# The feed-forward part's first steps set among the convolutions' second round

## The chip, the core and the metric

One core of a Trainium2 chip (trn2) runs the whole kernel. Its engines are TensorE (PE; weight loads are shown apart as PEld), VectorE (DVE), ScalarE (ACT), GpSimd (POOL) and SyncE (SP, which issues the transfers here). The metric is the device time of one execution in microseconds (us), as a median of runs. The program is written by hand: each engine has one list of instructions in a fixed order, and counting semaphores hold an instruction until another engine's is done.

## The reference, cut to what matters

Two layers over x of 4 x 512 x 128 float32. Each has an attention-like part and a feed-forward part, both behind a layernorm with a scale and a shift taken from a small vector (`mod`). The change touches the seam between layer 0's two parts, and the place where layer 1's expert weights are multiplied by a rotation.

```python
h = _layernorm(x) * (1 + ca) + sa
x = x + ga * _L0_attn_ref(h, ...)      # two long convolutions with gates, by way of FFTs
h = _layernorm(x) * (1 + cb) + sb
x = x + gb * _L0_ffn_ref(h, ...)
...
# _L0_ffn_ref
sim = einsum('bthn,hkpn->pbthk', h @ W_q, keys)              # 2 x 4 heads x 64 keys
(sx, sy), (ix, iy) = top_k(sim, 8)                           # 8 best of each side
scores, pk = top_k(sx[..., :, None] + sy[..., None, :], 8)   # 8 best of 64 pairs
w = silu(einsum('btd,bthkd->bthk', h, down_embed[indices]) * softmax(scores))
experts_states = einsum('bthk,bthkd->btd', w, up_embed[indices])
dense = silu(h @ W_up.T) @ W_down.T
return dense + experts_states
...
# _L1_ffn_ref, behind its experts
for i in range(3): moe_out = moe_out @ expm(gens[i])
```

## The kernel before

**The convolutions.** `convolutions_tensor`, `_scalar`, `_gpsimd` and `_vector` handle one batch of 512 rows (four tiles of 128). Two lanes run side by side; lane 0 takes batches 0 and 2, lane 1 takes 1 and 3, so there are two rounds. A batch is transposed, projected (L848), folded (L913, L914), transformed (L857), multiplied by the filter's spectrum (L920 to L925) and transformed back (L866), twice; then it is added to `x` (L938, L940). Lane 0 owns PSUM banks 4 and 5, lane 1 owns 6 and 7.

**The rotations.** `rotations_tensor`, `_scalar` and `_vector` form the matrix exponentials of layer 1. At their heart are 16 products of three matrices on PE (L639, twelve matmul passes each), and after each a DVE step (L778) and ACT copies (L621, L624) that the next product waits for. A last pair of products with copies between (L670, L783, L787; L674, L791) gives the rotation. Then PE multiplies the expert weights by it in four groups (L684, and L688 for the bias) in banks 0 and 1, and DVE copies each group out (L796, L799).

**The order.** Each engine's list is made by `together`, which takes one piece in turn from each of its streams (lane 0, lane 1, setup, rotations) until all are used up; `yield` ends a piece, and `idle(n)` skips n turns:

```python
def together(*streams):
    streams = list(streams)
    while streams:
        for s in list(streams):
            if next(s, StopIteration) is StopIteration:
                streams.remove(s)
```

No clock and no cost enters: the place of a step is where its turn falls. On the chip the lists run as fast as the semaphores let them.

**The feed-forward part** (`feed_forward_*`) starts when these streams are used up. Ahead of its loop over 16 tiles stands a head. DVE takes the statistics of batch 0 (`statistics`, L1278 to L1283), POOL normalises it (`normalised`, L1222, L1227), PE transposes it (`turned`, L980), DVE scales and shifts it into `hT` (`keep_turned`, L1287). PE forms tile 0's similarities (`sim`, L997), the dense half's four up-projections (`up`, L988) and tile 1's similarities; ACT copies the similarities (L1119) and applies silu (L1113). DVE then chooses for tile 0: `tops_of` (L1301, eight best of 64), `indices_of` (L1307, L1310), `best_of` (L1316 to L1325), `strike` (L1330) and `code_of` (L1334 to L1353). ACT's `exps` (L1123, L1125) and POOL's `past_of` (L1234 to L1249) serve the same choice. PE's `logit` (L1029) and `down` (L1004) follow, then in the loop `code` (L1011, L1013) and `rank` (L1022, L1023), whose result with ACT's exponential (L1135) DVE turns into weights in `gate_of` (L1362, L1364), four heads to a tile. In the loop's turn n DVE does `tops_of` and `indices_of` of tile n + 1 ahead of tile n's gates. PE's banks are SIM 4, GD 5, SUMS 6, OUT 7, RANK 0 and 1, LOGIT 2 and 3.

## Time and profile before

| | before |
|---|---|
| median of 3 runs | 1162.44 us (1161.05 to 1164.18) |
| the profiled execution's own time | 1161.96 us |
| its span, first to last instruction | 1160.7 us |
| mean granted TensorE clock | 0.987 of full |
| convolutions and rotations | to about 121 us |
| feed-forward of layer 0, first gate (L1362) | 144.03 us |

The times are those of whole executions; span and rows come from one profiled execution. A row of the timeline has a start, a duration, the engine, the program's line and the operation, `x12` for twelve instructions merged in one row, and in brackets how long the engine stood idle before and what released it. Matmuls are pipelined and the rows hold their modelled ends, so two rows on PE may overlap: the distance from start to start is what one costs in a full stream. A pair of passes makes one float32 matmul, hence `x2` and `x12`. PEclk in the windows is the clock granted to TensorE, 1.00 for 2.4 GHz and 0.50 for 1.2 GHz.

### The profile page before, as it was taken

The page shows a single profiled execution, that of the slowest core. Times are in us where ns is not written, and L with a number is a line of the kernel's source. Part 1 is how long each engine was busy: PE and PEld are TensorE (multiplying, and loading weights), DVE is VectorE, ACT ScalarE, POOL GpSimd, SP SyncE. Part 2 cuts the span into 40 slices and gives each one's busy share as a digit, 9 for nine tenths or more (in the row PEclk, how much of TensorE's full clock was granted, in tenths as well). Part 3 has the DMA queues.
Part 4 walks back from the last instruction along what each step waited for, and adds up shares of the span by engine and source line. Part 5 has one row for each costly group of instructions (what it writes and reads, how often), then busy time and mean ns, then how long its engine had stood idle before and what let it go on. Part 6 is the DMA issues. An engine that isn't in the chain of part 4 may idle for free.

```text
span 1160.7 us, 23183 instructions
## 1 busy us (share of the span) xinstructions
PE 1090.5 (94%) x7601; PEld 792.8 (68%) x7617; DVE 937.8 (81%) x3329; ACT 697.2 (60%) x1800; POOL 421.2 (36%) x707
## 2 busy tenths in 40 slices
PE   6798679999998999999999999999999999999997
PEld 5688446666666767777777777777776777656766
DVE  3988699999989599788888888888888898756767
ACT  1254345555566656777676767676767777745441
POOL 4400322233324135444444444444444555422310
PEclk9999889999999999999999999999999999999999
DMA  9200300000000000000000000000000000000000
GB/s 280 55 2 1 110 1 1 1 1 1 2 1 1 2 1 2 1 2 1 2 1 1 2 1 2 2 1 1 2 1 2 1 2 2 2 1 5 11 7 17
DMA packets 19957, 15.33 MB, mean 13 GB/s; under 512 B 2432, under 2 KB 18816, under 8 KB 19712
## 3 DMA queue, kind: packets, MB, share of 16 engines
q1 hardware_dynamic: 19840, 13.86, 4.1%
q8 instruction: 63, 1.03, 0.4%
q14 instruction: 54, 0.44, 0.1%
HBM read 12.81 MB, written 1.05 MB: 12 GB/s over the span
## 4 chain that ended last, share of the span: by engine, by line
PE 76%; DVE 13%; ACT 5%; issue 3%; POOL 1%; DMA 0%; SPq 0%; DVEq 0%; ACTq 0%; POOLq 0%
PE bank L1607 12%; PE bank L1637 11%; PE bank L1601 10%; PE bank L1556 8%; PE bank L1044 5%; PE bank L1945 5%; PE bank L1966 4%; PE bank L1577 3%; PE bank L1585 3%; PE bank L1029 3%; ACT prb L1672 2%; PE bank L639 2%; DVE prob L1362 1%; PE bank L1023 1%; PE bank L1004 1%
## 5 line engine op out<-in xcount | busy, mean ns | idle before, releaser
L1703 POOL TENSOR_SCALAR prb<-prb,rnorm 128x512 f32<-128x512 f32 (+3 forms) x512 | 270.4, 545 | 349.4 <-DVE rnorm L1793 349.3
L1672 ACT ACTIVATE prb<-prb,negmax 128x512 f32<-128x512 f32 (+3 forms) x512 | 280.9, 552 | 113.5 <-DVE negmax L1775 113.5
L1775 DVE CUSTOM_DVE_ANT_0 prb<-bank,mask 128x512 f32<-128x512 f32 (+3 forms) x512 | 218.7, 484 | 18.5 <-PE bank L1601 18.3
L1607 PE MATMUL bank<-ident,prb 128*128 128x128 f32 x1280 | 158.2, 275 | 3.4 <-POOL prb L1703 2.9
L1607 PEld LDWEIGHTS bank<-ident,prb 128*128 128x128 f32 x1280 | 139.6, 141 | 22.9 <-issue 12.0
L1637 PE MATMUL bank<-prbT,vv 128*64 128x512 f32 (+3 forms) x1024 | 152.0, 439 | 0.0
L1637 PEld LDWEIGHTS bank<-prbT,vv 128*64 128x64 f32 x1024 | 63.4, 137 | 82.4 <-issue 82.2
L1680 ACT ACTIVATE prbT<-bank 128x512 f32<-128x512 f32 x128 | 76.5, 598 | 62.0 <-PE bank L1607 60.1
L1784 DVE COPY prbT<-bank 128x512 f32<-128x512 f32 x128 | 87.8, 690 | 14.8 <-PE bank L1607 14.4
L1672 ACT ACTIVATION_READ_ACCUMULATOR prb<-prb,negmax 128x1 f32 x512 | 96.8, 189 | 0.0
L2003 ACT ACTIVATE h<-bank,eb1T 128x512 f32<-128x512 f32 x64 | 43.7, 687 | 53.8 <-PE bank L1945 53.6
L1135 ACT ACTIVATE prob<-bank,negbest 128x512 f32<-128x512 f32 x64 | 43.9, 686 | 46.5 <-PE bank L1029 46.4
L2140 DVE SCALAR_TENSOR_TENSOR moe<-bank,wde,moe 128x128 f32<-128x128 f32 x128 | 44.8, 350 | 28.5 <-PE bank L1966 24.5
L1029 PE MATMUL bank<-mpair,hT 128*128 128x512 f32 x128 | 67.2, 607 | 0.1
L1044 PEld LDWEIGHTS bank<-ident,prob 128*128 128x128 f32 x512 | 59.1, 192 | 7.1 <-ACT gT L1113 5.5
L1945 PE MATMUL bank<-hTm,ew 128*128 128x512 f32 x128 | 61.0, 606 | 2.3 <-ACT h L2003 1.9
L1966 PEld LDWEIGHTS bank<-ew2R,h 128*128 128x128 f32 x512 | 58.9, 192 | 4.8 <-issue 4.3
L1044 PE MATMUL bank<-ident,prob 128*128 128x128 f32 x512 | 60.4, 276 | 0.7 <-ACT gT L1113 0.7
L1966 PE MATMUL bank<-ew2R,h 128*128 128x128 f32 x512 | 59.7, 276 | 0.0
L1362 DVE SCALAR_TENSOR_TENSOR prob<-bank,prob 128x512 f32<-128x512 f32 x64 | 43.8, 684 | 19.3 <-PE bank L1023 19.3
L1793 DVE RECIPROCAL rnorm<-rowsum 128x2 f32<-128x2 f32 (+1 forms) x192 | 31.7, 165 | 27.7 <-ACT prb L1672 27.6
L1364 DVE SCALAR_TENSOR_TENSOR prob<-prob,rsum,bank 128x512 f32<-128x512 f32 x64 | 47.8, 748 | 2.3
(465 smaller groups left out, 2368.7 us busy)
## 6 DMA issues: line engine op xcount, KB each, us to landing
x<-in_x SPq DMA_DIRECT2D x2, 512.0 KB, 6.0
ew2T<-in_ew2T SPq DMA_DIRECT2D x1, 1024.0 KB, 7.7
ew<-in_ew SPq DMA_DIRECT2D x1, 1024.0 KB, 5.6
wq<-in_Wq SPq DMA_DIRECT2D x2, 512.0 KB, 5.1
wk<-in_Wk SPq DMA_DIRECT2D x2, 512.0 KB, 7.6
wv<-in_Wv SPq DMA_DIRECT2D x1, 1024.0 KB, 8.2
out<-res SPq DMA_DIRECT2D x16, 64.0 KB, 1.5
wmod<-in_wmod SPq DMA_DIRECT2D x2, 384.0 KB, 6.9
```

The costliest lines, as they stand in the source:

```text
L1029: T.matmul(LOGIT[h % 2][:, :], tokens(n), mpair[:, h, :, :].rearrange("p i j -> p (i j)"), start=True, stop=True).then_inc(ff_logit, 1)
L1044: last = T.matmul(SUMS[:, c * P:(c + 1) * P], prob[n % 3][:, h, c * P:(c + 1) * P], ident[:, :], start=(h == 0), stop=(h == PH - 1 and c < 3))
L1556: last = T.matmul(into[:, :], left[:, j % 4, :], right, start=(n == 0), stop=(n == 2))
L1601: last = T.matmul(s_of(j, s, i, qc), q[r, qc * P:(qc + 1) * P], k[r, 0:(qc + 1) * P], start=(n == 0), stop=(n == 2))
L1607: last = T.transpose(into[:, at + (qc - kc) * P:at + (qc - kc + 1) * P], prb[j % 2][:, i, p_at[qc] + kc * P:p_at[qc] + (kc + 1) * P], iden ...
L1637: last = T.matmul(BO[DH * i:DH * i + DH, kc * P:S], vv[j // 4 % 2][:, kc, (2 * g + i) % 4, mp, :], prbT[:, i, pt_at[kc]:pt_at[kc] + (NT - ...
L1672: A.activation(v, v, ACT.Exp, scale=-1.0, bias=negmax[j % 2][:, place[qc], i:i + 1], accum_out=rowsum[j % 2][:, place[qc], i:i + 1]).then_ ...
L1703: last = G.tensor_scalar(v, v, rnorm[j % 2][:, place[qc], i:i + 1], 1.0, ALU.mult, ALU.mult)
L1775: V.tensor_tensor_reduce(prb[j % 2][:, i, p_at[qc]:p_at[qc] + (qc + 1) * P], s_of(j, s, i, qc), mask[:, (NT - 1 - qc) * P:S], 1.0, LARGEST ...
L1784: V.tensor_copy(prbT[:, part // 2, pt_at[1]:pt_at[1] + 4 * P], turn_bank(j, part)[:, :]).then_inc(at_ptv, 1)
L1945: T.matmul(F01[j % 2][:, :], ew1[:, j // HC, (j % HC) * P:(j % HC + 1) * P], hTm[b % 2], start=True, stop=True).then_inc(mx_up, 1)
L1966: last = T.matmul(bank[2 + t % 2 * 4 + e // 4][:, (e % 4) * D:(e % 4 + 1) * D], h1[b % 2][:, e * HC + c, t * P:(t + 1) * P], ew2R[:, e, c, ...
```

## The change

The head of the feed-forward part becomes a fifth stream, `ahead`, of each engine's `together`; the rest is `main`. Into `ahead` go: batch 0's statistics, rows, transposes and `hT` (now made by ACT, L1200, not DVE), the similarities of tiles 0 and 1, the four up-projections with their silus, the whole choice of tile 0, and `tops_of` and `indices_of` of tile 1. They use banks 2 and 3 (`AHEAD`), free after setup. `main` starts with `logit(0, 0)` and `down(0)`. ACT, not DVE, copies the rotated expert weights out of PSUM, and PE waits for the copies at the first `rank`. Tile buffers change places so that what `ahead` writes lies outside of the lanes' memory, and `main` waits for each lane's last batch (`cv_done`) where it takes over its memory or banks.

```diff
@@ convolutions_vector
-            dve.did(V.tensor_tensor(x[:, b, :, :], x[:, b, :, :], w.pv[:, :, 0, :], ALU.add))
-            dve.settle()
+            V.tensor_tensor(x[:, b, :, :], x[:, b, :, :], w.pv[:, :, 0, :], ALU.add).then_inc(w.cv_done, 1)
+            V.wait_ge(w.cv_done, n0 + 1)
@@ rotations_scalar, at its end (rotations_vector loses the same copies, L794 to L799)
+            yield from idle(6)
+            for j in range(E1 * HC // 4):
+                A.wait_ge(ew2_ps, j + 1)
+                A.activation(ew2R[:, 2 * j:2 * j + 2, :, :], bank[j % 2][:, :].rearrange("p (e c d) -> p e c d", e=2, c=HC), ACT.Copy).then_inc(ew2_kept, 1)
+                yield
+            A.wait_ge(ew2_ps, E1 * HC // 4 + 1)
+            A.activation(eb2R[:, :], bank[0][0:E1, 0:D], ACT.Copy).then_inc(ew2_kept, 1)
@@ feed_forward_tensor
+            def ahead():
+                yield from idle(32)
+                T.wait_ge(keys_ready, 1)
+                T.wait_ge(pre.ln_xhat, 1)
+                for t in range(NT):
+                    last = T.transpose(AHEAD[0][:, t * P:(t + 1) * P], pre.xhat[:, t, :], ident[:, :])
+                last.then_inc(pre.ln_ps, 1)
+                yield from idle(2)
+                T.wait_ge(layer0_in, LAYER0_IN)
+                T.wait_ge(pre.h_ready, 1)
+                sim_ahead(0)
+                up_ahead(0)
+                yield from idle(2)
+                T.wait_ge(ff_simk, 1)
+                sim_ahead(1)
+                T.wait_ge(ff_silu, 1)
+                up_ahead(1)
+                yield from idle(2)
+                T.wait_ge(ff_simk, 2)
+                up_ahead(2)
+                T.wait_ge(ff_silu, 2)
+                up_ahead(3)
+                yield
...
+            def main():
+                T.wait_ge(const_ready, 3)
+                T.wait_ge(ff_silu, NT)
+                T.wait_ge(lanes[0].cv_done, B // 2)
+                logit(0, 0)
+                down(0)
+                for n in range(TILES):
...
+                    if n == 0:
+                        T.wait_ge(ew2_kept, E1 * HC // 4 + 1)
+                    rank(n, 0)
...
+                    if n == 0:
+                        T.wait_ge(lanes[1].cv_done, B // 2)
@@ feed_forward_scalar
+            def ahead():
+                yield from idle(33)
+                A.wait_ge(pre.ln_ps, 1)
+                A.activation(hT[0], AHEAD[0][:, :], ACT.Identity, bias=modT[0][:, 3, 0:1], scale=modT[0][:, 4, 0:1]).then_inc(pre.h_ready, 1)
+                yield from idle(2)
+                keep_sim(0)
+                silu_up(0, 0)
+                yield from idle(2)
+                keep_sim(1)
+                silu_up(0, 1)
+                yield from idle(2)
+                silu_up(0, 2)
+                silu_up(0, 3)
+                yield from idle(4)
+                exps(0)
+                yield
@@ feed_forward_gpsimd
+            def ahead():
+                yield from idle(28)
+                normalised(pre, 0, 0)
+                yield from idle(13)
+                past_of(0)
+                yield
@@ feed_forward_vector
+            def ahead():
+                yield from idle(27)
+                V.wait_ge(const_ready, 3)
+                V.wait_ge(rows_kept, len(ROWS))
+                statistics(pre, 0)
+                yield from idle(9)
+                tops_of(0)
+                yield from idle(2)
+                at = indices_of(0)
+                yield from idle(2)
+                cast = best_of(0, *at)
+                yield from idle(2)
+                strike(0)
+                yield from idle(2)
+                code_of(0, cast)
+                yield from idle(2)
+                tops_of(1)
+                yield from idle(2)
+                found_first.extend(indices_of(1))
+                yield
+
+            def main():
+                for n in range(TILES):
...
+                    if more and n:
+                        tops_of(n + 1)
...
+                        at = indices_of(n + 1) if n else found_first
@@ tensor_program (the other engines alike)
-            together(batches(convolutions_tensor, 0), batches(convolutions_tensor, 1), setup_tensor(), rotations_tensor())
...
-            last = feed_forward_tensor()
+            ff_ahead, ff_main, last = feed_forward_tensor()
+            together(batches(convolutions_tensor, 0), batches(convolutions_tensor, 1), setup_tensor(), rotations_tensor(), ff_ahead())
+            ff_main()
```

How the lists change, at three places. A row is one instruction or a run of equal ones, output`<-`inputs. The numbers behind names count buffers.

PE, second round, the first forward transforms of the two lanes and the squarings between them (L639 before, L648 now); before:

```order
L857 MATMUL bank<-fold_78,c_fwd_sb 128x128 x8
L848 MATMUL bank<-proj_w,hT_1_90 128x384
L639 MATMUL bank<-xm_e 128x128 x6
L857 MATMUL bank<-fold_86,c_fwd_sb 128x128 x8
L639 MATMUL bank<-xm_e 128x128 x6
L866 MATMUL bank<-spec_o_81,c_inv_sb 128x128 x8
L639 MATMUL bank<-xm_e 128x128 x6
```

and now, the same place, with the similarities (L1084) and up-projections (L1087) between:

```order
L859 MATMUL bank<-fold_78,c_fwd_sb 128x128 x8
L850 MATMUL bank<-proj_w,hT_1_90 128x384
L1084 MATMUL bank<-msim,hT_101 128x512
L1087 MATMUL bank<-hT_101,w_up 128x512
L648 MATMUL bank<-xm_e 128x128 x6
L859 MATMUL bank<-fold_86,c_fwd_sb 128x128 x8
L1084 MATMUL bank<-msim,hT_101 128x512
L1087 MATMUL bank<-hT_101,w_up 128x512
L648 MATMUL bank<-xm_e 128x128 x6
L868 MATMUL bank<-spec_o_81,c_inv_sb 128x128 x8
L1087 MATMUL bank<-hT_101,w_up 128x512 x2
L648 MATMUL bank<-xm_e 128x128 x6
```

A similarity and an up-projection stand between the transforms and each of two squaring products, and two up-projections ahead of a third.

DVE, from the squaring step before lane 0's last multiplication by the filter; before:

```order
L778 SCALAR_TENSOR_TENSOR xm_e<-bank,xm_over,xm_b_120 128x128 x3
L920 TENSOR_TENSOR spec_o_81<-spec_79,filt 128x512
L921 TENSOR_TENSOR spec_t_80<-spec_79,filt 128x512
L924 TENSOR_TENSOR spec_o_81<-spec_o_81,spec_t_80 128x256
L925 TENSOR_TENSOR spec_o_81<-spec_o_81,spec_t_80 128x256
L778 SCALAR_TENSOR_TENSOR xm_e<-bank,xm_over,xm_b_120 128x128 x3
```

and now, where L1392 to L1411 are `code_of(0)` and L922 to L927 are L920 to L925 of before:

```order
L787 SCALAR_TENSOR_TENSOR xm_e<-bank,xm_over,xm_b_120 128x128 x3
L1392 TENSOR_TENSOR chosen<-pair_r,pair 128x256
L1396 TENSOR_TENSOR xeq<-iota_x,topf 128x256
L1400 TENSOR_REDUCE cnt<-chosen 128x32
L1401 TENSOR_TENSOR ycode<-iota_y,topf 128x2048
L1404 TENSOR_TENSOR xeq<-xeq,cnt 128x256
L1406 TENSOR_REDUCE esum<-ebest 128x4
L1409 TENSOR_REDUCE xcode<-xeq 128x32
L1411 RECIPROCAL rsum<-esum 128x4
L922 TENSOR_TENSOR spec_o_81<-spec_79,filt 128x512
L923 TENSOR_TENSOR spec_t_80<-spec_79,filt 128x512
L926 TENSOR_TENSOR spec_o_81<-spec_o_81,spec_t_80 128x256
```

The eight instructions of the code stand ahead of lane 0's last filter product, on which its last inverse transform waits.

PE, from the rotated expert weights on; before:

```order
L684 MATMUL bank<-xm_b_121,ew2T 128x128 x16
L688 MATMUL bank<-xm_b_121,eb2T 8x128
L980 MATMUL bank<-ident,xhat_pre 128x128 x4
L997 MATMUL bank<-msim,hT_93 128x512
L988 MATMUL bank<-hT_93,w_up 128x512 x4
L997 MATMUL bank<-msim,hT_93 128x512
L1029 MATMUL bank<-mpair,hT_93 128x512
L1004 MATMUL bank<-downT,hT_93 128x512
L1011 MATMUL bank<-rank_ident,ycode 128x128 x16
L1013 MATMUL bank<-identb,xcode 128x128
```

and now:

```order
L693 MATMUL bank<-xm_b_121,ew2T 128x128 x16
L697 MATMUL bank<-xm_b_121,eb2T 8x128
L1032 MATMUL bank<-mpair,hT_101 128x512
L1007 MATMUL bank<-downT,hT_101 128x512
L1014 MATMUL bank<-rank_ident,ycode 128x128 x16
L1016 MATMUL bank<-identb,xcode 128x128
```

Transposes, both similarities and the up-projections are gone from behind the rotated weights; `logit`, `down` and the code follow at once.

## Rows read from the trace of the kernel before

**Rows 1.** The page's first part, whole span: busy time, share, instructions.

```profile
PE 1090.5 (94%) x7601; PEld 792.8 (68%) x7617; DVE 937.8 (81%) x3329; ACT 697.2 (60%) x1800; POOL 421.2 (36%) x707
```

**Rows 2.** Waits, 74 to 145 us: who waited for whom, us, times, longest.

```profile
PE bank L980 <- POOL xhat_pre L1227: 6.3, 1, 6.3
```

**Rows 3.** Windows: length, busy PE, PEld, DVE, ACT, POOL, PEclk, DMA, GB/s.

```profile
78.56:98.97 20.41, 20.28 (x151) 18.07 (x152) 15.68 (x42) 10.37 (x28) 0.00 (x0) 1.00 0.00 1
98.97:115.38 16.41, 13.48 (x119) 13.07 (x117) 14.18 (x36) 6.05 (x15) 0.00 (x0) 1.00 0.00 1
115.38:144.03 28.65, 20.02 (x79) 12.10 (x81) 17.86 (x99) 8.40 (x14) 8.71 (x12) 0.82 0.37 111
```

**Rows 4.** Timeline of PE, the loop: start us, us, what, [idle before it].

```profile
78.56 1.58 PE L639 MATMUL bank<-xm_e 128*128 128x128 f32 x12 [0.36 <-ACT xm_b L624]
...
88.96 1.50 PE L639 MATMUL bank<-xm_e 128*128 128x128 f32 x12
...
92.64 1.58 PE L639 MATMUL bank<-xm_e 128*128 128x128 f32 x12
...
95.84 1.50 PE L639 MATMUL bank<-xm_e 128*128 128x128 f32 x12
...
98.97 1.50 PE L639 MATMUL bank<-xm_e 128*128 128x128 f32 x12
...
115.38 5.46 PE L684 MATMUL bank<-xm_b,ew2T 128*128 128x128 f32 x32 [2.55 <-DVE xm_b L791]
```

**Rows 5.** Timeline of PE, behind the loop.

```profile
120.77 0.39 PE L688 MATMUL bank<-xm_b,eb2T 128*8 128x128 f32 x2
127.50 1.09 PE L980 MATMUL bank<-ident,xhat_pre 128*128 128x128 f32 x4 [6.34 <-POOL xhat_pre L1227]
...
136.04 1.02 PE L997 MATMUL bank<-msim,hT 128*128 128x512 f32 x2
136.90 1.02 PE L1029 MATMUL bank<-mpair,hT 128*128 128x512 f32 x2
137.76 1.02 PE L1004 MATMUL bank<-downT,hT 128*128 128x512 f32 x2
139.89 1.21 PE L1011 MATMUL bank<-rank_ident,ycode 128*128 128x128 bf16 x16 [1.11 <-DVE xcode L1351]
...
142.12 0.38 PE L1023 MATMUL bank<-sel_x,codeT 128*128 128x512 bf16 x1
```

**Rows 6.** Timeline of DVE, feed-forward's beginning up to the first gate.

```profile
135.34 0.59 DVE L1316 MAX8 best<-pair 128x8 f32<-128x64 f32 x4
...
136.15 0.09 DVE L1330 MATCH_VALUE_LOAD pair_r<-best,pair 128x8 f32 x1
...
137.04 0.47 DVE L1334 TENSOR_TENSOR chosen<-pair_r,pair 128x256 f32<-128x256 f32 x1
...
139.84 1.08 DVE L1301 MAX8 tops<-sim 128x8 f32<-128x64 f32 x8
...
142.13 0.41 DVE L1307 TENSOR_TENSOR pair<-tops 128x256 f32<-128x256 f32 x1
...
144.03 0.66 DVE L1362 SCALAR_TENSOR_TENSOR prob<-bank,prob 128x512 f32<-128x512 f32 x1
```

**Rows 7.** Timeline of DVE, the copy that releases the rotated weights.

```profile
115.04 0.28 DVE L791 COPY xm_b<-bank 128x128 f32<-128x128 f32 x1
```

**Rows 8.** L920 by itself: count, duration ns min/median/max, first and last start, forms.

```profile
L920 DVE TENSOR_TENSOR spec_o<-spec,filt x8: 681/688/843, 36.8 to 107.5; 128x512 f32<-128x512 f32 x8
```

**Rows 9.** Windows of 2 us around the rotated weights' start (columns as above).

```profile
112.00:114.00 2.00, 0.49 (x2) 0.30 (x2) 1.93 (x5) 0.15 (x1) 0.00 (x0) 1.00 0.00 0
114.00:116.00 2.00, 0.62 (x4) 0.62 (x5) 1.93 (x6) 0.00 (x0) 0.00 (x0) 0.96 0.00 0
116.00:118.00 2.00, 2.00 (x12) 2.00 (x11) 1.34 (x2) 0.00 (x0) 0.00 (x0) 0.50 0.00 0
118.00:120.00 2.00, 2.00 (x14) 2.00 (x14) 0.70 (x2) 0.00 (x0) 0.00 (x0) 0.69 0.04 8
```

More of the change, by code:

```diff
@@ L1103, in last @@
                     experts(TILES - 1)
-            return last
+            return ahead, main, last
         def feed_forward_scalar():
@@ L1214, in last @@
                     keep_sums(TILES - 1)
[L1216 removed]
+            return ahead, main, last
         def feed_forward_gpsimd():
@@ new lines, in main @@
+            def main():
+                for n in range(TILES):
+                    before, after = normed_at(n)
+                    more = n + 1 < TILES
+                    if more and n:
+                        tops_of(n + 1)
+                    if before is not None:
+                        statistics(pre, before)
+                    if after is not None:
+                        V.wait_ge(ff_res, NT * after + NT)
+                        statistics(post, after)
+                    if more:
+                        at = indices_of(n + 1) if n else found_first
+                    if n >= 2:
+                        result(n - 2)
+                    gate_of(n, 0)
+                    if more:
+                        cast = best_of(n + 1, *at)
+                    gate_of(n, 1)
+                    if more:
+                        strike(n + 1)
+                    gate_of(n, 2)
+                    gate_of(n, 3)
+                    if more:
+                        code_of(n + 1, cast)
+                    if before is not None:
+                        keep_before(before)
+                    if after is not None:
+                        keep_after(after)
```

275 lines of the change are left out of this document (111 added, 164 removed).

## The prediction

> **What bounds the kernel now.** I read the page first: PE is busy for 94% of the span and DVE for 81% [rows 1], so a gain has to come from a stretch in which PE stands still. The waits of the stretch around the change show one: from 74 to 145 us PE's longest single wait is 6.3 us for POOL's `xhat_pre` [rows 2], the head of the feed-forward part. The windows then split the stretch in three [rows 3]. From 78.56 to 98.97 us PE is busy for 20.28 of 20.41 us and DVE for 15.68: convolutions and squarings, bound by PE. From 98.97 to 115.38 PE is busy for 13.48 of 16.41 and DVE for 14.18: a changing bound. From 115.38 to 144.03 both have slack (20.02 and 17.86 of 28.65). That last stretch is a chain: the experts' rotated weights (L684, L688), DVE's copies of them, statistics, POOL's rows, transposes, hT, similarities, the choice of tile 0, its code. It ends with the first gate (L1362) of tile 0 at 144.03 us [rows 5, 6]. From there on DVE works without a gap through tile 0, so whatever moves this first gate moves everything behind it, and the time is settled by one question: when does that gate start?
>
> **The change, part by part.** The reckoning has three terms. I follow the squarings' products on PE (L639), which alternate with the convolutions at a period of 3.13 us (95.84 to 98.97 [rows 4]), and count how much later each part ends.
>
> Term 1, up to the product at 98.97. DVE gets the statistics of batch 0 in the middle of the loop, ahead of the batch-1 residual and of the next squaring step. Batch 1's statistics stand between the end of `tops_of` at 140.9 and 142.13 us [rows 6], 1.2 to 1.3 us. The product at 78.56 already had to wait 0.36 us [rows 4], so it comes later by nearly all of it: I take 1.2. PE gets four transposes, two similarities and four up-projections. A 512-column pair of passes takes 0.86 us from start to start at the full clock (136.04 to 136.90 [rows 5]); six are 5.2 us; the four transposes took 1.09 us at the low clock (127.50 [rows 5]), so half of that at the full one, of which I count 0.4 from start to start. That is 5.6 us on a PE that has no room. Little is hidden: of the intervals between products one was 3.68 us (88.96 to 92.64) and the next 3.20 (92.64 to 95.84) [rows 4], so some 0.5 us of PE waiting is filled. 1.2 + 5.6 - 0.5 = 6.3 us later at the twelfth product.
>
> Under this PE time the first `tops_of` and `indices_of` on DVE (1.0 and 1.9 us, from 139.84 to 140.84 and 142.13 to 144.03 [rows 6]) cost nothing: DVE had 20.41 - 15.68 = 4.7 us idle there [rows 3] and gets 5.6 more. Were PE's share smaller, they would cost up to 2.9. ACT takes hT, two similarity copies, four silus and a table load; it was busy for 10.37 of 20.41 us [rows 3], and a copy for the next product is needed only after a convolution's eight pairs of passes. I cost it at nothing.
>
> Term 2, from there to the start of the rotated weights, 115.38. Here DVE gets best (135.34 to 136.15, 0.8), strike (to 137.04, 0.9), the code (to 139.84, 2.8), `tops_of(1)` 1.0 and `indices_of(1)` 1.9 [rows 6]: 7.4 us. They stand in DVE's order ahead of the copies that release the rotations (L783, L787, L791), although those need nothing of them. DVE had 16.41 - 14.18 = 2.2 us idle here [rows 3]. 7.4 - 2.2 = 5.2 us later. PE's next product and the inverse transforms now wait for DVE, not the other way round. So the copy at 115.04 [rows 7] and with it L684 at 115.38 [rows 4] come 6.3 + 5.2 = 11.5 us later, at about 126.9.
>
> Term 3, from L684 to the first gate. Before it took 144.03 - 115.38 = 28.65 us [rows 3]. Now: the rotated weights to their end, 5.46 + 0.3 us (120.77 plus 0.3 is 121.1 [rows 5]), then `logit(0,0)` and `down(0)` at 0.86 each (136.04, 136.90, 137.76 [rows 5]), then tile 0's code, whose operands have long been ready: from L1011 at 139.89 to the end of the rank's second matmul at 142.50 [rows 5] and DVE's start, 2.7. That is 5.75 + 1.7 + 2.7 = 10.2 us, so 28.65 - 10.2 = 18.5 us less. DVE is through with its convolutions, the residual and batch 1's statistics some 7 us before this gate and waits; what it no longer copies for the rotated weights (ACT does it now, at much the same price) is therefore free but brings nothing. If DVE were late instead, each us would count.
>
> Sum without what the trace doesn't show: 6.3 + 5.2 - 18.5 = -7.0 us.
>
> Unknown cost one: POOL now normalises batch 0 (4 instructions and the power) and does `past_of(0)` beside DVE's convolutions; before, POOL did nothing from 78.56 to 115.38 us [rows 3]. Lower bound 0. For the upper one the convolutions' first round is the nearest: there alone POOL wrote rows beside DVE, and L920 took at most 843 ns against a median of 688 [rows 8]: 0.15 us each. With two to eight such meetings it is 0.3 to 1.2 us, part of it under PE's time; I take 0.5. The Trainium skill (SBUF — State Buffer, "Who interferes with whom") says more: a DVE instruction with two SBUF inputs and a GpSimd instruction that reads SBUF take the shared port in turn, and the second blocks fully until the first is done. By that rule each of four rows of POOL (0.8 us) could hold DVE up whole, 3 us in place of 0.5. The row of L920 speaks against so much, and I keep it as a rival.
>
> Unknown cost two: PE's clock. Before, the granted clock falls to 0.50 for 116 to 118 us, after PE was busy for only 0.49 and 0.62 us of the two windows ahead [rows 9]; so L684 began slow before, and the 5.46 us hold that already. Afterwards PE stands still for some 2.5 us while DVE finishes the code, and for about 5 us around the rotation's copies. The second pause is like the old one and priced; the first may lower the clock early. Its cost: nothing, or the following inverse transform and product (1.8 and 1.3 of the period of 3.13 us) at twice their time, less 0.5 us of slack, 2.6 us. I take nothing and put 2.6 into a rival. It could also turn out better: with the old 6.3 us pause gone the clock may stay up in tiles 0 and 1, where it fell before; that is worth 1 us at most.
>
> Sum: -7.0 + 0.5 = **-6.5 us**. The profiled execution took 1161.96 us (span 1160.7), 0.5 under the median of three, 1162.44. 1161.96 - 6.5 = 1155.5 us, which is 0.6% under that median. A measurement of this kernel can tell about 0.3%, 3.5 us.
>
> **The rivals.**
> (a) The early fall of the clock. For it: a pause of 3.3 us in busy work (112.8 to 115.38, with 0.5 us within) was enough before [rows 9]. Against it: the new first pause is shorter and has full work on both sides. Time: 1155.5 + 2.6 = 1158.1 us, still faster by 0.37%.
> (b) POOL and DVE in turn, as the skill's rule has it: four rows of 0.8 us and the products of `past_of(0)` block DVE, mostly where it is the bound. 3 to 4 us in place of 0.5: 1158.5 to 1159 us, at the edge of what can be told.
> (c) The streams wait for each other more than the sum has it: each engine's list is one fixed order, and the new steps wait across engines in it (PE for ACT's silu, ACT for POOL's `epair`, DVE for ACT's exponentials). One round of such a chain, DVE's 3.1 us period lost once, gives 1158.6, two give 1161.7: no difference that can be told. For it: the products of 3.13 us leave no room for a late copy. Against: by the rows each of these results is ready 1 to 4 us before it is asked for.
> (d) The other side, slower: PE at half its clock from the first DVE-bound pause until the first gate. Then both inverse transforms (1.8 each), the last product (1.3), the two rotation steps (0.6), the rest of the rotated weights (1.7 beyond the 5.46) and `logit`, `down` and the code (2.9) take their time once more: 10.1 us against 6.5, so 1165.6 us. It decides for a slower kernel as soon as the clock stays low for more than about two thirds of these 20 us. Against: before, the clock was on its way back from 118 to 120 us already, 0.69 in the mean [rows 9].
> (e) The change doesn't do what it says: if some wait held the early steps until the loop's end, the time would be as before, 1162. The order excludes most of that, since the new steps stand between the convolutions.
>
> **How the numbers follow.** Forecast (-6.5, from -10 to -5): 0.56. (a) 0.14, (b) 0.08, (c) 0.14, of which half under 0.3%, (d) and anything else slower 0.06, (e) 0.02. The time is that of the forecast, **1155.5 us**. The range goes down to 1151.0 (no price for POOL, more idle DVE time used, a clock that stays up: 4.5 us less) and up to 1160.5, taking in (a), (b) and one round of (c); out are (d), (e) and the worse half of (c), and a little below. Faster by over 0.3%: the forecast, (a), half of (b) and half of (c), about 0.80; within 0.3%: 0.14; slower: 0.06.
>
> **What would show it.** The products on PE should come about 6 us later at the twelfth and 9 to 10 us later at the last; L684's successor should start at 126 to 128 us, the first gate at 136.5 to 138.5 instead of 144.03, and DVE should wait about 7 us for it. After that every landmark should stand earlier by the same amount to the end of the span. The POOL rows beside DVE should be 0.8 to 1.2 us each; L920's successor near 0.69 to 0.85. The granted clock at about 116 to 120 us decides (a) and (d). The prediction is wrong if the gate comes before 134 us (then DVE's order did not hold the rotations back), or after 141 (a wait the sum lacks), or if the head start is lost again later in the feed-forward part.

## The result, and the profile after

The changed kernel takes 1156.61 us as a median of 20 runs (1154.97 to 1162.55), the kernel before, on the same chip, 1163.18 us (1160.71 to 1164.88, 20 runs). The ratio is 0.9955, 95% interval 0.9943 to 0.9967: 5.2 us less, between 3.8 and 6.6 (the two medians stand 6.6 us apart). The profiled execution of the changed kernel took 1160.07 us (span 1158.8), 3.5 us over its own median, so it can't be set against the old profile by its total. It can be by landmarks. I count from one product on PE that stands ahead of the change's first step in every list: at 72.42 us before, at 74.67 now. What lies ahead of it is the same list of instructions, and what moved there belongs to the execution (last section). Where the prediction speaks of the twelfth product (98.97 us before), it is the thirteenth of sixteen; I keep its name.

The page's first part, whole span, to set beside [rows 1]:

```profile
PE 1095.0 (94%) x7617; PEld 797.6 (69%) x7617; DVE 933.8 (81%) x3323; ACT 699.9 (60%) x1806; POOL 422.5 (36%) x707
```

No share moved by more than a point; for a change in one stage the page's shares say nothing. The windows of the three stretches do, cut at the same steps as [rows 3]:

```profile
81.89:107.25 25.36, 25.36 (x166) 20.59 (x167) 18.79 (x72) 15.26 (x35) 2.33 (x4) 1.00 0.00 1
107.25:131.53 24.28, 15.81 (x118) 14.86 (x117) 22.65 (x80) 7.75 (x18) 4.06 (x5) 0.92 0.00 1
131.53:141.63 10.10, 10.10 (x61) 7.83 (x62) 2.56 (x12) 4.32 (x9) 4.17 (x5) 0.85 0.30 88
```

The first stretch grew from 20.41 to 25.36 us and PE is busy in all of it. The second grew from 16.41 to 24.28, and DVE is busy for 22.65 of it: DVE is the bound there. The third, from the rotated weights to the first gate, shrank from 28.65 to 10.10 us, all PE.

The timeline of PE in the loop, to set beside [rows 4]:

```profile
81.89 1.58 PE L648 MATMUL bank<-xm_e 128*128 128x128 f32 x12 [1.44 <-DVE xm_e L787]
...
94.44 1.50 PE L648 MATMUL bank<-xm_e 128*128 128x128 f32 x12
...
99.29 1.50 PE L648 MATMUL bank<-xm_e 128*128 128x128 f32 x12
...
104.13 1.50 PE L648 MATMUL bank<-xm_e 128*128 128x128 f32 x12
...
107.25 1.50 PE L648 MATMUL bank<-xm_e 128*128 128x128 f32 x12
...
119.62 2.61 PE L868 MATMUL bank<-spec_o,c_inv_sb 128*128 128x128 f32 x16 [3.35 <-DVE spec_o L927]
122.02 2.62 PE L648 MATMUL bank<-xm_e 128*128 128x128 f32 x12
124.47 1.95 PE L868 MATMUL bank<-spec_o,c_inv_sb 128*128 128x128 f32 x16
...
131.53 5.34 PE L693 MATMUL bank<-xm_b,ew2T 128*128 128x128 f32 x32 [2.55 <-DVE xm_b L800]
```

The products now follow each other at 4.85 and 4.84 us where similarities and up-projections stand between, and at the old 3.12 (104.13 to 107.25) where none does. Then comes what was not there before: PE waits 3.35 us for DVE's L927, and what follows runs slowly (2.61 and 2.62 us where a transform and a product in full stream have 1.95 and 1.50).

PE behind the loop, to set beside [rows 5], and the first gate on DVE:

```profile
136.80 0.39 PE L697 MATMUL bank<-xm_b,eb2T 128*8 128x128 f32 x2
137.12 1.12 PE L1032 MATMUL bank<-mpair,hT 128*128 128x512 f32 x2
138.08 1.02 PE L1007 MATMUL bank<-downT,hT 128*128 128x512 f32 x2
138.94 1.14 PE L1014 MATMUL bank<-rank_ident,ycode 128*128 128x128 bf16 x16
...
141.54 0.38 PE L1026 MATMUL bank<-sel_x,codeT 128*128 128x512 bf16 x1
```

```profile
141.63 0.69 DVE L1420 SCALAR_TENSOR_TENSOR prob<-bank,prob 128x512 f32<-128x512 f32 x1 [7.44 <-PE bank L1026]
```

The 6.3 us wait for POOL [rows 2] is gone, the head's chain too; DVE now waits 7.44 us for PE ahead of the gate.

Why PE paused for 3.35 us stands in two timelines, first DVE's, then POOL's:

```profile
116.25 0.66 DVE L922 TENSOR_TENSOR spec_o<-spec,filt 128x512 f32<-128x512 f32 x1
116.83 1.12 DVE L923 TENSOR_TENSOR spec_t<-spec,filt 128x512 f32<-128x512 f32 x1
117.98 0.83 DVE L926 TENSOR_TENSOR spec_o<-spec_o,spec_t 128x256 f32<-128x256 f32 x1
118.73 0.83 DVE L927 TENSOR_TENSOR spec_o<-spec_o,spec_t 128x256 f32<-128x256 f32 x1
...
121.87 0.68 DVE L923 TENSOR_TENSOR spec_t<-spec,filt 128x512 f32<-128x512 f32 x1
122.58 0.43 DVE L926 TENSOR_TENSOR spec_o<-spec_o,spec_t 128x256 f32<-128x256 f32 x1
```

```profile
116.47 0.93 POOL L1289 TENSOR_TENSOR chosen_past<-chosen,past 128x256 f32<-128x256 f32 x1 [7.55 <-DVE rsum L1411]
117.48 1.05 POOL L1295 TENSOR_TENSOR zpast<-epair,chosen_past 128x256 f32<-128x256 f32 x1
118.61 0.67 POOL L1298 TENSOR_TENSOR zpast<-zpast,rsum 128x256 f32<-128x256 f32 x1
```

Three DVE rows take 1.12, 0.83 and 0.83 us, the same instructions 5 us later 0.68, 0.43 and 0.42: 1.25 us more. POOL's L1289 takes 0.93 us; its median over 16 tiles is 0.63. Both engines pay. And the clock, in windows of 2 us:

```profile
118.00:120.00 2.00, 0.38 (x3) 0.39 (x4) 2.00 (x4) 0.00 (x0) 1.20 (x2) 1.00 0.00 0
120.00:122.00 2.00, 2.00 (x15) 2.00 (x15) 2.00 (x12) 0.00 (x0) 0.00 (x0) 0.73 0.00 0
122.00:124.00 2.00, 2.00 (x12) 2.00 (x11) 1.31 (x3) 0.38 (x1) 0.00 (x0) 0.50 0.00 0
```

The granted clock goes to the 1.2 GHz level as PE works again: it is 1.00 in the window of the pause and 0.50 two windows on.

**All profiles in one table.** The first number is the time of the product I count from; the others are distances from it: the first gate, the choice (`best_of`) in tiles 3, 14 and 15, the end of the span. Here "before" and "after" are the kernels of the study, each profiled more than once; the others are the experiments below.

| profile | product at | gate | tile 3 | tile 14 | tile 15 | end |
|---|---|---|---|---|---|---|
| before | 72.42 | 71.61 | 105.86 | 277.38 | 294.33 | 1088.3 |
| before_again | 72.42 | 71.61 | 105.90 | 277.37 | 297.21 | 1091.5 |
| before_third | 72.51 | 71.64 | 105.89 | 277.42 | 294.37 | 1088.3 |
| after | 74.67 | 66.96 | 99.78 | 271.28 | 289.85 | 1084.1 |
| again | 71.42 | 67.02 | 99.85 | 271.33 | 289.92 | 1084.2 |
| after_third | 73.10 | 67.88 | 100.67 | 272.19 | 290.77 | 1085.0 |
| after_fourth | 76.33 | 67.57 | 100.91 | 272.46 | 289.42 | 1083.3 |
| e_copies_dve | 72.45 | 66.45 | 99.82 | 271.66 | 290.24 | 1084.6 |
| e_pool_late | 71.33 | 65.58 | 99.16 | 270.63 | 287.58 | 1081.6 |
| e_warm | 73.13 | 66.70 | 99.87 | 271.34 | 288.29 | 1082.1 |
| e_choice_late | 72.47 | 59.86 | 93.12 | 264.57 | 281.53 | 1075.4 |
| e_best | 72.01 | 58.00 | 91.96 | 263.45 | 280.41 | 1074.5 |

The old kernel's three profiles agree to 0.05 us up to tile 14. The changed kernel is ahead by 4.65 us at the gate in its first profile (3.7 to 4.7 in all four), by 6.1 at tile 3 (5.0 to 6.1), and holds that to tile 14.

### The profile page after: what moved, and what is told of

It reads as the page before. It is cut to its first block, busy times and chain, and to the rows that moved or that the text cites. A ratio compares the mean times of both kernels' runs of the same rounds, so it can differ in the third digit from the quotient of the medians.

```text
span 1158.8 us, 23194 instructions
## 1 busy us (share of the span) xinstructions
PE 1095.0 (94%) x7617; PEld 797.6 (69%) x7617; DVE 933.8 (81%) x3323; ACT 699.9 (60%) x1806; POOL 422.5 (36%) x707
## 4 chain that ended last, share of the span: by engine, by line
PE 76%; DVE 14%; ACT 5%; issue 3%; POOL 1%; DMA 0%; SPq 0%; DVEq 0%; POOLq 0%
PE bank L1683 12%; PE bank L1713 10%; PE bank L1677 10%; PE bank L1632 7%; PE bank L1047 5%; PE bank L2021 5%; PE bank L2042 4%; PE bank L1653 3%; PE bank L1661 3%; PE bank L1032 3%; ACT prb L1748 2%; DVE prob L1420 2%; PE bank L648 1%; PE bank L1025 1%; PE bank L1007 1%
## 5 line engine op out<-in xcount | busy, mean ns | idle before, releaser
L1289 POOL TENSOR_TENSOR chosen_past<-chosen,past 128x256 f32<-128x256 f32 x16 | 10.4, 648 | 107.9 <-DVE rsum L1411 107.9
```

## The experiments

**again: the changed kernel once more.**

> The changed kernel once more, for a second profile. Its twenty executions lie in two groups, twelve from 1154.97 to 1157.12 us and eight from 1159.0 to 1162.55; the profiled one (1160.07) belongs to the upper. Theory: the lower group is the sum of the prediction (1155.5), and the upper one adds the early fall of the clock (2.6 us) and a start-up that came 2.2 us later (in that profile the product before the change's first step starts at 74.67 us, not 72.42). If this profile is of the lower group, the granted clock stays at 1.00 from 112 to 124 us relative to a loop that starts as before, and the first gate stands at 137 to 138 us. Rival: both groups have the same clock at that place and differ later, in the feed-forward part or in attention.

Measured: 1156.42 us (1154.62 to 1160.61, 12 runs), ratio 0.9944 (0.9927 to 0.9960). Its profiled execution took 1156.88 us and shows the same fall of the clock behind the same 3.35 us pause, and the gate 67.02 us behind the product. The theory of this run failed: that fall is not what sets these two executions apart. Their times differ by 3.2 us, and the product I count from stands 3.25 us apart, so all of it lies ahead of the change.

**e_pool_late: POOL's second half of tile 0 behind the convolutions.**

```diff
@@ feed_forward_gpsimd, past_of
+                if n == 0:
+                    G.wait_ge(lanes[1].cv_done, B // 2)
                 G.wait_ge(ff_rsum, n + 1)
```

> POOL's three products of past_of(0) wait until lane 1's convolutions are over, so that DVE's L922 to L927 of lane 0 run without POOL beside them. Theory (the two engines take turns at a port): these four take 2.0 us in place of 3.2 (0.66, 1.12, 0.83, 0.83 in the changed kernel), everything behind comes 1.2 us earlier, and PE's pause there shrinks from 3.35 us to about 2.1, so the clock falls there less often: 1.2 to 3.8 us faster than the changed kernel, 1152 to 1155 us. Rival (the longer rows are DVE's own, from its operands): no change.

Measured: 1155.20 us (1154.17 to 1160.16, 6 runs), ratio 0.9934 (0.9908 to 0.9960). In its profile, DVE at the same place, then PE's pause, then the windows of that place and of the rotated weights:

```profile
113.50 0.68 DVE L923 TENSOR_TENSOR spec_t<-spec,filt 128x512 f32<-128x512 f32 x1
114.21 0.42 DVE L926 TENSOR_TENSOR spec_o<-spec_o,spec_t 128x256 f32<-128x256 f32 x1
```

```profile
115.03 2.05 PE L868 MATMUL bank<-spec_o,c_inv_sb 128*128 128x128 f32 x16 [2.10 <-DVE spec_o L927]
```

```profile
116.00:118.00 2.00, 2.00 (x20) 2.00 (x19) 1.97 (x9) 0.38 (x1) 0.00 (x0) 1.00 0.00 0
126.00:128.00 2.00, 2.00 (x11) 2.00 (x11) 1.92 (x10) 0.36 (x1) 0.98 (x2) 0.50 0.03 8
```

With POOL away the DVE rows are 0.68 and 0.42 again, PE's pause is 2.10 instead of 3.35 us, the whole 1.25, and the clock holds. That POOL lengthened the rows and the pause is shown; that the shorter pause kept the clock up is not, for in e_copies_dve below it also stays up behind 3.35 us. The rotated weights start 2.7 us earlier (54.20 us behind the product, 56.86 in the changed kernel), 1.25 of it from POOL and 1.4 from the clock, but take 6.62 us instead of 5.34. So 1.4 us are gained at the gate, and 0.6 are left at tile 3 (99.16 against 99.78). The total lies at the upper edge of what was expected and moved by less than a measurement can tell.

**e_choice_late: DVE's second half of the choice behind the convolutions.**

```diff
@@ feed_forward_vector, ahead
                 cast = best_of(0, *at)
                 yield from idle(2)
-                strike(0)
-                yield from idle(2)
-                code_of(0, cast)
-                yield from idle(2)
-                tops_of(1)
-                yield from idle(2)
-                found_first.extend(indices_of(1))
+                found_first.append(cast)
                 yield
@@ main
+                strike(0)
+                code_of(0, found_first.pop())
                 for n in range(TILES):
...
-                    if more and n:
+                    if more:
                         tops_of(n + 1)
...
-                        at = indices_of(n + 1) if n else found_first
+                        at = indices_of(n + 1)
```

> DVE's strike, code of tile 0, tops and indices of tile 1 (0.9 + 2.8 + 1.0 + 1.9 = 6.6 us) stand behind the convolutions' last residual, where DVE waited 7.44 us for the first gate; PE's order is untouched. Theory (in the loop's second half DVE's order holds the rotations back): the rotated weights start 4.5 to 5.5 us earlier against the same loop start, the gate as much, 1150 to 1152 us. Rival (PE's 5.6 us of added work sets the loop's end, DVE's steps ride along): the same time as the changed kernel, or 2 us more since DVE now ends only 0.6 us before the gate.

Measured: 1148.95 us (1147.92 to 1153.48, 5 runs), ratio 0.9878 (0.9848 to 0.9907): clear of the changed kernel by over 7 us. PE at the end of the rotations, and the gate:

```profile
119.07 0.49 PE L683 MATMUL bank<-xm_e,xm_b 128*128 128x128 f32 x2 [0.38 <-DVE xm_b L796]
122.10 5.46 PE L693 MATMUL bank<-xm_b,ew2T 128*128 128x128 f32 x32 [2.55 <-DVE xm_b L800]
```

```profile
132.33 0.69 DVE L1420 SCALAR_TENSOR_TENSOR prob<-bank,prob 128x512 f32<-128x512 f32 x1 [1.01 <-PE bank L1026]
```

The twelfth product stays where it was (32.57 us behind the product counted from, 32.58 in the changed kernel), the last comes 4.7 us earlier (42.70 against 47.35), and the rotated weights start 7.2 us earlier (49.63 against 56.86). The theory was right and its 4.5 to 5.5 us too low. The four steps of the choice (strike, code, tops and indices) take 6.6 us, of which old idle time of DVE hid 1.9; the collision with POOL (1.25) and the clock behind the pause (1.33) went with them, 7.3 in all. Behind the convolutions they cost nothing: DVE had 7.4 us of waiting there and still has 1.0. The 2.55 us ahead of the rotated weights were there before the change too [rows 4]: DVE has a residual and lane 1's last products between the two copies.

**e_warm: work on PE in the pause.** Twenty products that nobody reads, placed ahead of the inverse transform that waits.

```diff
@@ feed_forward_tensor, ahead
                 up_ahead(3)
+                yield from idle(7)
+                T.wait_ge(ff_silu, NT)
+                for _ in range(20):
+                    T.matmul(AHEAD[1][:, 0:P], ident[:, :], ident[:, :], start=True, stop=True)
                 yield
```

> Twenty products of the identity with itself into a free bank stand on PE between the fifteenth squaring and lane 0's last inverse transform, 2.2 us of work at the full clock in a pause of 3.35. Theory (the pause lowers the clock, and the inverse transform and the last product then take 2.41 and 2.45 us from start to start in place of 1.79 and 1.34): the granted clock stays at 1.00 there, both take their full-speed time, the gate comes 1 to 2.5 us earlier than in a profile with the fall, and the upper group of executions becomes rarer. Rival (the fall there is hidden, since DVE is behind anyway): rows at full speed but the same times.

Measured: 1155.69 us (1154.68 to 1157.27, 6 runs), ratio 0.9929 (0.9905 to 0.9952), as the changed kernel. None of the six lies in the upper group, too few to say that it became rarer. The twenty products are not 2.2 us of work but twice that, since each is a pair of passes:

```profile
114.78 4.41 PE L1084 MATMUL bank<-ident 128*128 128x128 f32 x38
```

They outlast the pause, and the inverse transform starts 0.95 us later than in the changed kernel (45.90 against 44.95 us behind the product). The windows at the held place and at the rotated weights, and those weights on PE:

```profile
120.00:122.00 2.00, 2.00 (x20) 2.00 (x20) 1.78 (x4) 0.38 (x1) 0.00 (x0) 1.00 0.00 0
128.00:130.00 2.00, 0.79 (x3) 0.79 (x4) 1.93 (x5) 0.00 (x0) 0.00 (x0) 0.50 0.00 0
```

```profile
129.21 5.87 PE L693 MATMUL bank<-xm_b,ew2T 128*128 128x128 f32 x32 [2.55 <-DVE xm_b L800]
```

The clock stays up through the transform and the product, and DVE's wait for the product goes from 1.33 to 0.54 us, although the transform starts late. But then the clock is down from the next pause on, the rotated weights take 5.87 instead of 5.34 us, and at tile 3 nothing is left (99.87 against 99.78). How much of this is the 0.95 us of the filling itself, this run alone can't tell; e_copies_dve below has the clock up without any filling, and there nothing is left at tile 3 either.

**e_best: fewer columns on PE in the loop.** On top of e_choice_late, three of tile 0's four up-projections stand in PE's pause of 2.55 us; their banks alternate for that (`AHEAD[c % 2]` where `AHEAD[c == 2]` was), and their silus stand later in ACT's order.

```diff
@@ feed_forward_tensor, ahead (and e_choice_late's edits)
                 T.wait_ge(ff_simk, 1)
                 sim_ahead(1)
-                T.wait_ge(ff_silu, 1)
-                up_ahead(1)
-                yield from idle(2)
+                yield from idle(16)
                 T.wait_ge(ff_simk, 2)
+                up_ahead(1)
+                T.wait_ge(ff_silu, 1)
                 up_ahead(2)
...
@@ feed_forward_scalar, ahead
                 keep_sim(1)
+                yield from idle(14)
                 silu_up(0, 1)
-                yield from idle(2)
                 silu_up(0, 2)
                 silu_up(0, 3)
-                yield from idle(4)
                 exps(0)
```

> This is the kernel with tile 0's strike and code and tile 1's tops and indices back behind the convolutions (1148.95 us), and with three of tile 0's four up-projections moved from the convolutions' full stretch on PE into PE's pause between the last squaring product and the rotated weights. Theory: in the loop PE is the bound, and each pair of 512 columns costs 0.86 us there, in the pause nothing: the rotated weights start 2.6 us earlier against the last product of before the change's steps, and the time is 1146.4 us. With columns in the pause the clock may stay up as the rotated weights start (before the change they began at 0.50): then 5.46 becomes 4.4 us and the time 1145.4. Rival A: DVE, not PE, sets the second half also without tile 0's code; then the products in the loop come at the same times and the time stays at 1149. Rival B: the moved projections stand in the way of the rotation's last two steps, which wait behind them on PE, and the silus behind them delay the copies of the rotation on ACT: the 2.6 us are given back, 1148 to 1150.

Measured: 1149.08 us (1147.82 to 1149.83, 4 runs), ratio 0.9882 (0.9861 to 0.9903). It beats both kernels of the study; that it beats e_choice_late can't be told. In its profile:

```profile
117.36 2.84 PE L1087 MATMUL bank<-hT,w_up 128*128 128x512 f32 x6
120.07 2.05 PE L693 MATMUL bank<-xm_b,ew2T 128*128 128x128 f32 x16
123.21 2.05 PE L693 MATMUL bank<-xm_b,ew2T 128*128 128x128 f32 x16 [1.09 <-ACT ew2R L637]
```

The projections fill the pause exactly, and the clock stays up. The rotated weights start 1.6 us earlier, not 2.6: PE waits 0.52 us for DVE's L927 and 0.60 for L916 between products now that its columns are gone, so DVE is the next bound. Then PE waits 1.09 us for ACT, whose copies stand behind three silus, a table load (1.28 us) and the exponentials. At the gate 1.9 us are gained, 1.1 at tile 14. The theory's 1146.4 us and its 2.6 us were not reached; the time is that of rival A, and the profile shows a part of each rival.

**e_copies_dve: the rotated weights' copies back on DVE**, the one part undone that the prediction costed at nothing.

```diff
@@ rotations_vector, at its end (rotations_scalar loses the same copies)
+            for j in range(E1 * HC // 4):
+                yield
+                V.wait_ge(ew2_ps, j + 1)
+                V.tensor_copy(ew2R[:, 2 * j:2 * j + 2, :, :], bank[j % 2][:, :].rearrange("p (e c d) -> p e c d", e=2, c=HC)).then_inc(ew2_kept, 1)
...
```

> One part of the change undone: the rotated expert weights are again copied out of PSUM by DVE, all else as in the changed kernel (1156.5 us). Theory: DVE waits 7.4 us for the first gate in the changed kernel, the copies (about 0.4 to 0.7 us each, four of them and a small one) fit into that, and the moved copies brought nothing: 1156.5 us within 1. Rival: the copies now stand behind DVE's statistics or residual and release the banks late, so that the rotated weights on PE take longer and the first gate comes 1 to 3 us later: 1157.5 to 1159.5.

Measured: 1158.13 us (1156.12 to 1161.55, 10 runs), ratio 0.9957 (0.9939 to 0.9975), which takes in the changed kernel's 0.9955. The gate stands 66.45 us behind the product (66.96 in the changed kernel), tile 3 at 99.82 (99.78): the same. The median lies in the range of the rival, 1.5 us over the changed kernel's, but the ratio shows no difference, and the gate did not come late. Moving the copies to ACT brought nothing that the gate shows, as long as DVE waits for it (2.59 us here). The profile holds a second thing:

```profile
117.39 2.05 PE L869 MATMUL bank<-spec_o,c_inv_sb 128*128 128x128 f32 x16 [3.35 <-DVE spec_o L928]
```

```profile
118.00:120.00 2.00, 2.00 (x20) 2.00 (x20) 2.00 (x11) 0.38 (x1) 0.00 (x0) 1.00 0.00 0
```

The same pause of 3.35 us, and here the clock did not fall. DVE does not wait for the last product at all, where it waits 1.33 us in `after`, and the rotated weights start 1.43 us earlier (55.43 us behind the product, 56.86). So this prices the fall: about 1.3 us at that wait. It came back in the next pause, where the clock fell, and the rotated weights took 6.25 us for 5.34.

**before_again: the old kernel's second profile.**

> The kernel before once more, for a second profile of it. The distance from the product ahead of the change's first step (72.42 us in the first profile) to the first gate (144.03) should be 71.6 us within 0.3, if that distance is a property of the program and not of one execution; the product itself may stand up to 3 us elsewhere, since the start of an execution varies. Rival: the distance varies by 1 us or more, in which case differences of that size between kernels say nothing.

Measured: 1165.16 us. The gate stands 71.61 us behind the product, as in the first, so differences of half a microsecond there can be read between kernels. But its span is 3.2 us longer, and 2.9 of that lie between tiles 14 and 15. First `before`, then `before_again`, each with the window and with PE's row behind its pause there:

```profile
355.00:360.00 5.00, 4.32 (x33) 3.84 (x34) 5.00 (x21) 3.14 (x6) 1.36 (x2) 1.00 0.02 5
...
355.68 1.12 PE L1004 MATMUL bank<-downT,hT 128*128 128x512 f32 x2 [2.86 <-DVE prob L1364]
```

```profile
355.00:360.00 5.00, 4.33 (x14) 3.30 (x15) 5.00 (x21) 3.14 (x6) 1.36 (x2) 0.50 0.01 2
...
355.67 2.08 PE L1004 MATMUL bank<-downT,hT 128*128 128x512 f32 x2 [2.86 <-DVE prob L1364]
```

The same kernel, the same pause of 2.86 us at the same time, and in one execution the clock falls there, in the other not.

**after_third, after_fourth, before_third: is that fall the execution's or the kernel's?**

> The changed kernel a third time, for its profile. Two profiles of it show the granted clock low at 350 to 360 us, between tiles 14 and 15, which costs 1.6 us there; the first profile of the kernel before has the low clock at 410 to 420 us and pays nothing at tile 15, the second has it at 355 to 365 us and pays 2.9 us. Theory: where the clock falls late in layer 0 is chance, of the execution and not of the kernel, so a profile with a time near 1155 us shows it at 400 to 410 us and nothing paid at tile 15, and one near 1158 to 1160 us shows it at 350. In both the distance from the product ahead of the change's first step to the choice in tile 14 is 271.3 us within 0.1. Rival: the change itself brings the clock down at 350 us; then this profile shows it there as well, whatever its time.

> As the run before it: the changed kernel once more. Theory: low clock either at 350 (1.6 us at tile 15) or at 400 us (nothing), with the time higher or lower by as much; start-up moves the whole by up to 3 us besides. Rival: always at 350.

> The kernel before a third time. Theory: low clock at either of the two places; from the product at 72.42 to the first gate 71.6 us again, to the choice in tile 14 277.4 us. A profile near 1161 us has it at 410, one near 1164 us at 355 us. Rival: the time differs without the clock's late fall, through the start.

Measured: 1159.38, 1160.96 and 1162.12 us. after_third has it at 350 us and pays 1.6 at tile 15; after_fourth has it at 410 and pays nothing (tile 14 to 15: 16.96 us, against 18.57 in `after`); before_third is as the first profile of the old kernel. So it is the execution's. What failed is the tie to the total: after_fourth, without the loss at tile 15, is the slowest of the four, through 3.9 us ahead of the change. And tile 14 stands at 272.2 and 272.5 us, not at 271.3: so 0.9 to 1.2 us differ there between executions of the changed kernel. In after_third they stand at the gate already; in after_fourth 0.6 stand at the gate, the rest comes between tiles 1 and 2.

## Why the prediction was right, and where its parts were not

**Term 1: 6.3 us forecast, 6.03 measured** (the twelfth product 32.58 us behind the product counted from, 26.55 before). It holds part by part. The statistics: the product behind them comes at 4.10 us (77.79 to 81.89) where 3.02 was, 1.08 for 1.2. Transposes: an interval of 3.28 became 3.71, 0.43 for 0.4. Similarities and up-projections: 3.77, 3.68 and 3.20 became 5.49, 4.85 and 4.84, together 4.53 for 5.2 less 0.5. `tops_of` and `indices_of` of tile 0 on DVE cost nothing, as costed.

**Term 2: 5.2 us, and 0.5 for POOL, forecast; 7.87 measured.** This is the step that was mis-sized. DVE did become the bound ahead of the rotations, and e_choice_late shows it. Of the 7.4 us of DVE steps, best (0.8) ran before the stretch began, so 6.6 lie in it. Idle time fell from 2.23 to 1.63 us, of which 1.33 is a wait of another kind: for a product at the low clock. Added up: 6.6, + 1.25 for POOL on L923, L926 and L927, + 0.6 of other DVE work in the stretch (0.3 of it L915 beside POOL's L1283), - 1.9 of old idle time filled, + 1.33 for the clock = 7.9. That the 1.33 is the clock's price shows in e_copies_dve, where the clock stayed up and DVE did not wait there. So the two unknown costs were both taken too low: POOL's 0.5 against 1.25, or 1.55 with L915 (above the upper bound of 1.2), the clock's 0 against 1.3.

**POOL beside DVE.** The bound came from L920 at 843 ns beside POOL's rows of the first round [rows 8]. Those are `xhat` rows with one tensor input; `past_of` has POOL instructions with two, and they held DVE's for up to 0.44 us each. The row of L920 also spoke for DVE's side alone. POOL's own `xhat` rows in the trace of the kernel before, first while DVE did next to nothing (9 to 16 us), then beside DVE's rows in the convolutions' first round, tell the rest (count, ns min/median/max):

```profile
L818 POOL TENSOR_SCALAR xhat_lane<-x,mv_lane,rstd_lane x8: 787/792/797, 9.0 to 15.5; 128x128 f32<-128x128 f32 x8
L818 POOL TENSOR_SCALAR xhat_later<-x,mv_later,rstd_later x8: 794/1172/1782, 35.9 to 45.5; 128x128 f32<-128x128 f32 x8
```

Beside DVE a row of POOL took up to 1 us more, where L920 took 0.16 more: the price showed on POOL's side, and I had looked at one side only. The page of the Trainium skill that the prediction set against the row (SBUF — State Buffer, "Who interferes with whom") describes this well: POOL's L1289, 0.63 us alone, took 0.93 since L922 was under way, and then L923 ended 0.55 us behind it, L926 0.28 us behind L1295 and L927 0.28 behind L1298, as if each had waited for the other's instruction. By the trace the rule was right and my reading of the row was not; what rival (b) had too high, 3 to 4 us, was the number of meetings: POOL's rows of batch 0 at 81 us held up no DVE row that I found on the path. The DVE rows beside them read one input out of PSUM (L787, L909) and took 0.87 and 0.55 us, as before the change.

**The clock.** The prediction costed the first pause at nothing and gave the early fall 2.6 us in rival (a). The pause came out at 3.35 us, since POOL lengthened it by 1.25, and in all four profiles of the changed kernel the clock fell behind it. So rival (a) happened. In `after` it cost 1.3 us at the next wait of DVE, half of its price. Where the clock stayed up (e_warm, e_copies_dve), 0.3 and 0.5 us were left of that at the gate and nothing at tile 3.

**Term 3: 10.2 forecast, 10.10 measured**; the start of the rotated weights came late by term 2, not by this.

**The head start grew, and was to stay.** At the gate it was 4.65 us for 6.5. The prediction let the clock in tiles 0 and 1 bring "1 us at most"; it brought 1.4. These are the windows behind the gate, first of the kernel before, then of the changed one:

```profile
152.42:156.42 4.00, 2.47 (x19) 2.27 (x19) 3.96 (x15) 0.24 (x1) 1.98 (x3) 0.62 0.01 2
156.42:160.42 4.00, 4.00 (x8) 1.44 (x7) 3.27 (x20) 1.00 (x3) 0.00 (x0) 0.53 0.00 0
```

```profile
150.67:154.67 4.00, 3.11 (x19) 2.43 (x20) 3.96 (x22) 0.55 (x2) 1.98 (x3) 0.62 0.01 2
154.67:158.67 4.00, 4.00 (x13) 1.63 (x11) 3.79 (x21) 1.44 (x3) 0.42 (x1) 0.95 0.00 0
```

Before, the clock stayed at half for another 4 us. That goes with a head start of 6.1 us from tile 3 on, and up to tile 14 it is kept to 0.03 us, as forecast. At tile 15 the first profile loses 1.6 of it by the late fall, which belongs to the execution.

**The prediction's own signs.** It called itself wrong if the gate came after 141 us, and in `after` the gate stands at 141.63, in after_fourth at 143.90. Of this 2.25 and 3.91 us lie ahead of the change. Put on the old kernel's start, 72.42 us plus the table's distance, the gate stands at 139.4 to 140.3 us in the four profiles: below that limit, but above the 136.5 to 138.5 us forecast. The last product came 11.3 us later, for 9 to 10 forecast, and the rotated weights at 129.3, for 126 to 128; both misses are term 2's. DVE's wait was about the 7 us forecast.

So the forecast of 1155.5 us stands 1.1 under the median, with its mechanisms right but with two opposite errors inside: about 1.9 too much at the gate and about 1.4 too little behind it. That it came so near is partly luck. Of the rivals, (a) happened, at half its price. (b) happened in mechanism but not in size. (c) has no sign: no wait of DVE for ACT, of PE for silu or of ACT for `epair` stands on the path. (d), the clock down through the whole stretch, came nearest in after_third, where the granted clock was 0.50 from 118 to 122 us and the last product came 1.2 us later than in `after`; (e) is excluded by the table.

## What to carry to other kernels

When work is moved into a stretch with a shorter bound, move it only as far as the engine there has idle time: PE's columns and the first half of the choice could go into the loop for 6 us, and the second half on DVE, ahead of copies on which everything later hung, cost 7 us with what it brought along, while the place it came from had room for it. Where VectorE and GpSimd will meet, read the rows of both engines in the nearest stretch in which they met before: here VectorE's row showed 0.15 us and GpSimd's, in the same place, up to 1 us. And two profiles should be compared by distances from a landmark that the change doesn't touch, not by their totals: here the totals of one kernel's profiles differ by 4 us where the distances agree to a tenth or, in the changed part, to about 1 us.

## What the runs showed of the hardware

The clock falls in one execution and not in another, in the same list of instructions and behind the same pause. Ahead of the change, PE pauses 1.4 us for L916's fold in every profile; this is the row behind it in `after`, then in `again`:

```profile
29.53 3.78 PE L859 MATMUL bank<-fold,c_fwd_sb 128*128 128x128 f32 x16 [1.38 <-DVE fold L916]
```

```profile
28.05 2.05 PE L859 MATMUL bank<-fold,c_fwd_sb 128*128 128x128 f32 x16 [1.39 <-DVE fold L916]
```

It took 1.7 us more in `after` and `after_fourth`, at a granted clock of 0.50 from 30 to 34 us where `again` has 1.00, and in these two the product I count from comes late (74.67 and 76.33 us against 71.3 to 73.1 in the others). Behind the pause of 3.35 us it fell in four profiles of five, behind the one of 2.86 us at 355 us in one of the old kernel's three. Each such place is worth 1 to 3 us, and a few of them are of the size of the spread between executions of the changed kernel, 8 us. Of its first 20 executions all eight at 1159 us and above have a mean granted clock of 0.983 to 0.987, all twelve below 1157.2 us one of 0.988 or more. What decides it in an execution, the runs leave open.

The clock falls just ahead of the rotated weights or as they start in every profile but that of e_best, where PE has full work through the pause ahead of them. They took 5.3 to 5.5 us in the old kernel, `after`, `again`, after_third and e_choice_late, and 5.9 to 6.6 in after_fourth and in all three that had kept the clock up through the pause before (e_pool_late, e_warm, e_copies_dve). In those last three the rotated weights started 0.8 to 2.7 us earlier and took 0.5 to 1.3 us longer: a clock kept up in one pause gave back more than half of what it had brought in e_warm and e_copies_dve at the next. Why, the runs leave open.
